# A metaformer layer on one core: the third scaling of a batch's logits at the end of step 6 instead of step 2

## The reference, cut to what matters

```
x  = x + conv(ln_c(x))             # ln_c: norm over the 64 channels of each pixel ("first norm")
     conv(v): v + w2 @ relu(w1 @ groupnorm8(v) + b1) + b2     # 1x1 convolutions, 8 groups
t  = tokens(x)                     # (8, 16384, 64)
t  = t + ffn(ln_t(t))              # ln_t: norm over the 64 channels again ("second norm")
     ffn(v): logits = v @ gate_w.T + gate_b; softmax over the 16384 pixels;
             per batch and expert (32): the 8 largest, their rows pooled, a two-layer
             expert network, and its output added back to those 8 rows
```

## Time and profile before

| | us |
|---|---|
| median of 3 runs | 597.01 (593.67 to 597.5) |
| the profiled execution | 596.93 |
| its span | 594.8 |
| PE busy | 471.5 (79%) |
| DVE busy | 468.2 (79%) |
| ACT busy | 421.4 (71%) |
| POOL busy | 272.9 (46%) |

### The profile page before, as it was taken

The page is one execution under the profiler, slowest core; times in us unless marked ns, Lnnn a source line. Parts: engine busy times, 40 slices in busy tenths (PEclk is TensorE's granted clock), DMA queues, the critical chain, the costliest instruction groups (busy, mean ns, idle before and its releaser), DMA issues.

```text
span 594.8 us, 12859 instructions
## 1 busy us (share of the span) xinstructions
PE 471.5 (79%) x4964; PEld 191.1 (32%) x4964; DVE 468.2 (79%) x830; ACT 421.4 (71%) x645; POOL 272.9 (46%) x340
## 2 busy tenths in 40 slices
PE   6767799989988997889789888887887776756810
PEld 1322333333333332333233233332332222346510
DVE  7845775898699879988997898789979997796300
ACT  3765799899879977999799978985875475650200
POOL 1027370344009324833471456145777682014774
PEclk9659999999889989999999998898988896775955
DMA  7995477867656865786477746651127821010000
GB/s 283 349 422 190 140 248 255 280 212 218 214 207 213 238 214 188 219 257 250 158 237 229 280 146 212 213 213 72 72 83 203 233 79 71 1 42 6 14 13 8
DMA packets 36475, 106.85 MB, mean 180 GB/s; under 512 B 5176, under 2 KB 6200, under 8 KB 32320
## 3 DMA queue, kind: packets, MB, share of 16 engines
q1 hardware_dynamic: 34368, 105.00, 52.2%
q0 software_dynamic: 2048, 1.05, 1.0%
HBM read 71.95 MB, written 34.08 MB: 178 GB/s over the span
## 4 chain that ended last, share of the span: by engine, by line
PE 33%; DVE 31%; issue 13%; ACT 12%; POOL 8%; DMA 1%; DVEq 0%; ACTq 0%; POOLq 0%
PE st L430 8%; POOL out_rows L1730 5%; PE tl L478 5%; ACT junk L882 5%; PE cv L441 5%; DVE xs L1101 4%; PE tl L457 4%; PE cv L449 4%; DVE top_i L1192 4%; DVE lg L1089 4%; DVE cnd L1187 4%; DVE tok L1108 4%; POOL xs L1628 3%; PE bc L552 3%; DVE us L1093 2%
## 5 line engine op out<-in xcount | busy, mean ns | idle before, releaser
L1628 POOL TENSOR_TENSOR xs<-xs,us 128x1024 f32<-128x1024 f32 x64 | 151.0, 2379 | 104.7 <-DVE gsum L1093 41.3
L1101 DVE SCALAR_TENSOR_TENSOR xs<-cv,vecs,xs 128x1024 f32<-128x1024 f32 x64 | 82.0, 1281 | 19.4 <-PE cv L449 18.9
L449 PE MATMUL cv<-hid,w2bd 64*64 64x512 f32 x512 | 73.1, 643 | 19.2 <-ACT hid L828 18.8
L828 ACT ACTIVATE hid<-cv,b1n 128x1024 f32<-128x1024 f32 x64 | 70.9, 1108 | 21.1 <-PE cv L441 20.8
L441 PE MATMUL cv<-us,w1n 64*64 64x512 f32 x512 | 72.1, 635 | 10.4 <-DVE xs L1101 10.3
L1108 DVE STREAM_TRANSPOSE tok<-xs 128x1024 f32<-128x1024 f32 x64 | 79.5, 1241 | 0.7
L1093 DVE CUSTOM_DVE_ANT_0 us<-us,bc 128x1024 f32<-128x1024 f32 x60 | 72.6, 1211 | 3.9 <-PE bc L552 2.4
L478 PE MATMUL tl<-xs,gcen 128*32 128x256 f32 x1024 | 74.9, 414 | 0.8 <-ACT us L835 0.8
L882 ACT ACTIVATE junk<-us 128x1024 bf16<-128x1024 f32 x64 | 67.5, 1054 | 3.5 <-DVE gsum L1093 1.8
L858 ACT ACTIVATE sqx<-xs 128x1024 f32<-128x1024 f32 x64 | 66.4, 1049 | 2.1 <-PE st L430 1.9
L552 PE MATMUL bc<-rstd_s,spread 32*128 32x256 f32 x368 | 48.5, 342 | 21.5 <-DVE lg L1089 7.4
(11 more groups left out here) (254 smaller groups left out, 647.8 us busy)
## 6 DMA issues: line engine op xcount, KB each, us to landing
us<-in_raw SPq DMA_DIRECT2D x64, 512.0 KB, 5.1
xs<-in_x SPq DMA_DIRECT2D x32, 1024.0 KB, 4.9
out_rows<-tok SPq DMA_DIRECT2D x64, 512.0 KB, 4.8
us<-in_e_w SPq DMA_DIRECT2D x8, 260.0 KB
xs<-in_e_w SPq DMA_DIRECT2D x8, 256.0 KB
sqc<-out_rows,idx_all POOLq DMA_INDIRECT x32, 3.0
out_rows<-sqc,idx_all POOLq DMA_INDIRECT x32, 2.1
vecs<-in_b SPq DMA_DIRECT2D x4, 0.2 KB, 6.8
```

The costliest lines, as they stand in the source:

```text
L449: mm = pe.matmul(cv[C * h:C * h + C, CH * sl:CH * sl + CH], w2bd[r, r], hid[r, CH * h:CH * h + CH], start=True, stop=True)
L828: nc.scalar.activation(hid[:], cv[:], ACT.Relu, bias=b1n[:, par:par + 1]).then_inc(h_done, 1)
L1101: nc.vector.scalar_tensor_tensor(out=xu, in0=cv[:], scalar=vecs[:, 3:4], in1=xu, op0=ALU.add, op1=ALU.add).then_inc(x1_done, 1)
L1628: nc.gpsimd.tensor_tensor(xu, xu, su, ALU.add).then_inc(s_done, 1)
```

## The change

One entry of the table moves: job L2 of iterations 1 to 6 stands at (6, 2), behind S7, and no longer at (2, 1), behind L1. Everything else is as it was, iteration 7 included.

```
-L_JOBS = {(1, 2): 0, (2, 0): 1, (2, 1): 2, (7, 0): 3}
+L_JOBS = {(1, 2): 0, (2, 0): 1, (6, 2): 2, (7, 0): 3}
```

## The result

| | before | changed |
|---|---|---|
| median, us | 593.72 (588.91 to 597.79, 20 runs) | 600.0 (595.61 to 603.4, 20 runs) |
| the profiled execution, its span | 596.93, 594.8 | 602.18, 600.1 |
| mean granted clock of that span | 0.899 | 0.894 |

The changed kernel takes 1.0091 times as long (95% interval 1.0061 to 1.0121): it is slower, by about 5.4 us (0.0091 of 593.72; the medians lie 6.3 us apart), and so by less than the 1% from which the prediction counts a kernel as slower. Against the profiled execution of before, on which the sum was made, the forecast was +5.8 and the profile shows +5.25.

The account below looks back on a forecast made before the run. The prediction took a chain of waits, not a full engine, as the bound: in step 3 x1 waits for conv2, in step 7 L3 is on it. 596.93 + 4.6 direct + 1.2 clock = 602.7 us, range 597.5 to 607.5.

Parts of the forecast that it names:

- the rival in which each L2 gives back its 1.13 us: Steps 2 to 5 run at DVE's pace, ACT's wait hides the rest in step 6: -6.8 us, 590.1; chance 0.05.
- The gain of step 3: Without L2, S0's spread starts when conv1 ends: 0.13 us earlier in iterations 1 to 5, 0.65 us; nothing counted for iteration 6.
- Step 6: L2 behind S7 waits 0.60 us for its spread and takes 1.13; turn 1.80 us late, 5.2 us passed on in all.
- the rival that hid it: Nearly no change, about 598, chance 0.27; one case: L2's spread always ready, no hand-off wait in step 6, +1.8 us.
- the cover: DVE's wait for ACT's last square before the second reduction, 1.01 us in iteration 3, 5.6 us in all, absorbing added delay.
- What is queued behind: Work behind the moved L2, such as conv1 of step 7, SP's store and POOL's additions, has room: counted at nothing.
- The clock: Idle time moving on PE changes falls of the granted clock in steps 3 and 7: net +1.2 us, bounded by +6 and -4.9.
- three falls in iterations 2 to 5, at 1.5 us each: Granted-clock falls in step 3 after PE's longer idle piece before conv1: +4.5 us.
- the joined wait: PE's two waits in step 2, before L2's spread and before conv1, become one of 1.7 to 2.0 us.
- two falls fewer of three in step 7: PE's wait for L3 shrinks from 1.37 to 1.1 us, removing two clock falls in iterations 1 to 5: -3.3 us.
- the direct cost: Loss in step 6 less gain in step 3, without clock effects: 5.2 - 0.65 = +4.6 us.
- the joined wait costs more: Rival: four clock falls come in step 3 and none goes in step 7, 607.5 us; chance 0.18.

Follow-up runs that it names:

- Run 9: The changed kernel with L1 of iterations 1 to 6 also moved, from ahead of x1 to behind it in step 2: 592.38 us, 0.9949 times before.
- run 2: The kernel before with L2 of iterations 1 to 6 multiplied by a constant tile at the end of step 6, no spread or hand-off: 596.58 us, 1.0055.
- run 3: The changed kernel with L2's multiplication in step 6 cut to four columns, spread and waits kept: 592.18 us, 0.9962 times before.
- Run 4: The changed kernel with L2's four matmuls also kept on PE at their old place in step 2, result unused: 599.63 us, 1.0103 times before.
- run 6: The changed kernel with four unread 128x256 matmuls on PE ahead of the group norm's sums, iterations 1 to 6: 598.98 us, 1.0069 times before.
- run 1: The kernel before with L2 of iterations 1 to 6 left out, spread and multiplication: 597.59 us, 1.0042 times before.
- run 8: The changed kernel with two unread matmuls, 128x256 and 128x128, ahead of the group norm's sums, iterations 1 to 6: 597.25 us, 1.0085 times before.
- run 10: As Run 9, but L2 spread at the end of step 5 and multiplied right behind the turn of step 6: 598.32 us, 1.0038 times before.
- run 7: The kernel before with two unread matmuls, 128x256 and 128x128, ahead of the group norm's sums, iterations 1 to 6: 590.63 us, 0.9947.
- run 5: The kernel before with four unread 128x256 matmuls on PE ahead of the group norm's sums, iterations 1 to 6: 596.63 us, 1.0016.
- run 11: Run 9 with the two unread matmuls of run 7 added: 590.8 us, 0.9940 times before.
- run 12: run 10 with the two unread matmuls of run 7 added: 591.07 us, 0.9975 times before.

## Why the prediction was right, and where it was not

**What bounds: right.** In step 3 x1 waits for conv2 and not for DVE; 0.69 us idle was measured for 0.8 forecast, and the rival in which each L2 gives back its 1.13 us fell. Run 9 is its counterpart: one place earlier DVE is the bound, and there the same instruction was worth 1.13 us. The Trainium skill, Perfetto Trace Analysis, section Identifying the Most-Contended Engine, would relieve the fullest engine first; by these runs, taking DVE's 1.13 us away gave 0.18 us in one place and 1.13 in the next.

**The gain of step 3: right in kind, too small.** 0.65 us forecast, 0.90 measured (0.18 in each of five, not 0.13). I let S0's spread start when conv1's record ends, 1.09 us behind its start; it starts at 1.02, since the records of PE overlap (conv1's ends at 239.07, the spread's starts at 239.00).

**Step 6: right, a little too large.** The turn came 1.83 us later for 1.80, the hand-off was 0.60 us as worked out, and the rival that hid it is out by the profile after and runs 2 and 3. The Trainium skill, Perfetto Trace Analysis, section Optimizing Tensor Performance, has matmul groups rotate through different PSUM banks for this reason, and the 0.60 us agree. What passed on was 4.64 us, not 5.2: the two reductions, which started 1.13 us apart before (263.93 and 265.06, the second waiting), now start 0.04 apart, so that the cover was near 0.1 us longer in each iteration than the 1.01 I read. From one undisturbed iteration to the next the kernel loses 0.51 us where I had said about 0.7.

**What is queued behind: right.** Conv1 of step 7 starts behind L2's spread and holds nothing up, and L3's spread was ready.

**The clock: the sum near, the places wrong.** This is the step that failed. I forecast "three falls in iterations 2 to 5, at 1.5 us each" behind the joined wait: none came there in the changed kernel. In iteration 3 the wait of 1.65 us passed at 1.00, in the other three a fall one step earlier, which cost nothing, had taken the wait away. Run 4, which splits the wait again, is no faster that can be told, and behind the four such waits of run 6 there was no fall either. I forecast two falls fewer of three in step 7, for 3.3 us: it was one, for 1.1. And for iteration 6, of which I said "I count nothing", the joined wait was 2.95 us and the low clock behind it cost 1.25 us up to x1 of step 3 and 0.35 up to that of step 4, and a fall ahead of x1 of step 6 another 1.56: 3.2 us in all, less the 1.1 of step 7. Net +1.2 forecast, +2.0 to 2.1 measured. That the sum came out is luck in part: a loss that I put into four iterations stood in one that I left out, and the direct cost, 0.9 us too large (4.6 for 3.7), made up for a clock term 0.9 us too small. The rival "the joined wait costs more" has some support all the same, though not in the change: without L2 anywhere (run 1), one of three waits of 1.65 us was followed by a fall worth 1.67, and so was one of three in run 3. Over all the profiles (the change and runs 1, 2, 3, 6 and 8) iterations 2 to 5 have sixteen such waits, and those two falls.

**The level.** The forecast of 602.7 stood on a profiled execution of 596.93; in the comparison the kernel before had a median of 593.72, so the change came out at 600.0 with nearly the forecast difference. Twenty runs of the kernel before lie between 588.91 and 597.79 us, a wider spread than this change, and the time goes with the mean clock.

**Open.** Which wait brings a fall and which not is not settled: waits of 1.45 to 1.46 us in one kernel (run 10) were followed by 1.00 twice and by less than 0.6 three times, waits of 0.95 us by a fall in two iterations of five in the changed kernel and in run 4 and in none in run 9, and falls in step 5 (run 8, iteration 4) have no long wait of their own that the profile shows. In runs without a profile only the mean clock is known, so how many falls they had, and where, is argued from it and not shown.

## What to carry to other kernels

A moved instruction is worth what the chain at its old place gives back and costs what the cover at its new place leaves over: read both from the idle times in brackets there, never from the busy shares. Two costs that a wait of 1.01 us hid singly (0.60 us whole, 1.13 us all but 0.04) did not fit together; add them before you compare them with the cover. When an engine's wait moves, follow the granted clock behind it: here taking work out altogether made the kernel slower (run 1), and 0.9 us of work that nobody reads made it faster (run 7).

## What the runs showed of the hardware

- A fall of the granted clock has the price of its place: 1.64 us behind L3's wait, 1.67 in step 3 (run 1), about 1.55 in step 5 (x1 to x1 of 7.56 for 6.01, run 8), and next to nothing where the next x1 waits for DVE (the fall in step 2 of iteration 5 in the changed kernel: from x1 to x1 8.47 us, as without).
- In step 7 of iterations 1 to 5 PE stands idle ahead of the group norm's sums, five times in each of the fourteen profiles. Of the 20 waits of 1.2 to 1.5 us (before, runs 1, 2 and 10) ten were followed by a fall, of the 15 of 0.95 us (the change, runs 4 and 9) four, of the 35 of 0.62 us down to nothing (runs 3, 5 to 8, 11 and 12) none.
- Four dead matmuls of 128x256 in f32 took 2.0 us of PE; two, of 256 and 128 columns, 0.9 by the records. In PE's wait for L3 (1.37 us) the two delayed nothing; the four outlasted it and put off x1 by 0.32 us.
